# State's product of the next tile made beside the own token's products, and y gated straight from its bank

## What is computed

```python
y_intra = einsum('bclmgr,bclmge,bcmgerp->bclgep', sg, dg, xgc) + einsum('bclmgr,bclmge,bcmgerp->bclgep', sb, dg, xbc)
_, Sprev = scan(lambda S, (cd, s): (cd[..., None, None] * S + s, S), zeros, (cdec, st))
y_inter = SCALE * einsum('bclgn,bclge,bcgenp->bclgep', Cc, dec_in, Sprev)
y = (y_intra + y_inter).reshape(B, T, D_INNER)
y = _rms(y * silu(z))
return y @ W_out
```

## Time and profile before

| what | value |
|---|---|
| median of three runs | 249.6 us (249.55 to 250.18) |
| the profiled execution, whole | 250.03 us |
| its span on the core | 248.2 us |
| mean granted clock of TensorE | 0.978 |
| busy share of the span: PE, DVE, ACT, POOL | 88%, 84%, 76%, 65% |
| set-up before the loop of tiles | 0 to 43 us |
| loop of tiles | 43 to 222 us |
| FFN of the last rounds and the output | 222 to 248 us |

### The profile page before, as it was taken

The page is one execution under the profiler, slowest core; times in us unless marked ns, Lnnn a source line. Parts: engine busy times, 40 slices in busy tenths (PEclk is TensorE's granted clock), DMA queues, the critical chain, the costliest instruction groups (busy, mean ns, idle before and its releaser), DMA issues. The chain is left out here.

```text
span 248.2 us, 6592 instructions
## 1 busy us (share of the span) xinstructions
PE 218.3 (88%) x1962; PEld 159.9 (64%) x1962; DVE 208.9 (84%) x646; ACT 188.6 (76%) x728; POOL 160.3 (65%) x275
## 2 busy tenths in 40 slices
PE   0895998679999999999999999999999999999930
PEld 0893443456767666768777876877687768657920
DVE  1789999987779988986999899989989997956880
ACT  2366776669988699877988798789779977989661
POOL 7433134757798698776769686968686866563530
PEclk9999799999999999999999999999999999999985
DMA  5980000000000000000000001000100110010123
GB/s 121 228 275 4 3 0 0 1 3 1 3 3 3 0 3 1 3 0 5 1 3 0 3 3 45 3 0 1 46 3 1 23 23 0 3 44 4 42 50 87
DMA packets 10199, 6.45 MB, mean 26 GB/s; under 512 B 864, under 2 KB 9856, under 8 KB 10160
## 3 DMA queue, kind: packets, MB, share of 16 engines
q1 hardware_dynamic: 10016, 5.77, 9.6%
q0 software_dynamic: 144, 0.21, 0.4%
HBM read 3.88 MB, written 2.10 MB: 24 GB/s over the span
## 5 line engine op out<-in xcount | busy, mean ns | idle before, releaser
L978 PE MATMUL bank<-x,sg 64*64 64x256 f32 x256 | 35.0, 391 | 0.6 <-DVE sg L1393 0.6
L1386 DVE TENSOR_TENSOR x<-bank,wx 128x512 f32<-128x512 f32 x32 | 21.9, 685 | 15.5 <-ACT bank L672 12.5
L672 ACT ACTIVATE bank<-bank,rsn 128x512 f32<-128x512 f32 x32 | 21.1, 658 | 17.0 <-PE bank L879 17.0
L978 PE MATMUL bank<-xg,sg 64*64 64x256 f32 x256 | 33.0, 376 | 0.0
L966 PE MATMUL pair<-x,turned_bc 64*64 64x256 f32 x224 | 29.6, 376 | 0.0
L544 POOL TENSOR_TENSOR y<-ysum,zs 128x256 f32<-128x256 f32 x32 | 23.8, 742 | 5.5 <-DVE ysum L1409 5.5
L455 POOL TENSOR_TENSOR rb<-mse,halfn 128x2 f32<-128x2 f32 x32 | 23.7, 741 | 2.5
L452 POOL TENSOR_TENSOR mse<-msb,eps_all 128x2 f32<-128x2 f32 x32 | 8.1, 253 | 25.5 <-ACT junk L663 25.4
L1071 PE MATMUL bank<-wo_sb,yt 128*128 128x128 f32 x128 | 22.7, 300 | 0.0
L1386 DVE TENSOR_TENSOR xg<-bank,wx 128x512 f32<-128x512 f32 x32 | 21.8, 680 | 0.0
L427 POOL TENSOR_TENSOR x_lo<-xnT_all,x_hi 128x128 fp32r<-128x128 f32 x32 | 14.7, 460 | 10.4 <-ACT x_hi L587 10.4
(11 more groups left out here) (195 smaller groups left out, 750.2 us busy)
## 6 DMA issues: line engine op xcount, KB each, us to landing
x_all<-x SPq DMA_DIRECT2D x16, 128.0 KB, 4.1
out<-o_all SPq DMA_DIRECT2D x14, 128.0 KB, 2.6
cm<-consts SPq DMA_DIRECT2D x1, 640.0 KB, 6.3
w_sb<-w_in SPq DMA_DIRECT2D x1, 480.0 KB, 4.0
out<-o_all SPq DMA_DIRECT2D x4, 64.0 KB, 2.1
cm<-consts POOLq DMA_DIRECT2D x1, 128.0 KB, 4.0
wo_sb<-w_out SPq DMA_DIRECT2D x1, 128.0 KB, 4.7
bcb_sb<-bc_bias SPq DMA_DIRECT2D x1, 96.0 KB, 4.6
```

What stands on the lines that cost most here:

```text
L672: nc.scalar.activation(x_ps[:], x_ps[:], ACT.Silu, scale=rsn[:, par:par + 1]).then_inc(S["x_silu"], 1)
L978: mm = nc.tensor.matmul(y_ps[half(h)], sg[half(h), a, r], rx(x, r)[half(h)], start=start, stop=stop)
L1386: vec.tensor_tensor((x1, xg)[a][:, par].rearrange("p (a e) -> p a e", e=P), x_ps[:].rearrange("p (a e) -> p a e", e=P), wx[:, par, a].unsq ...
```

## The change

Three things are changed, in the path that runs:

1. The state's product of tile n + 1 is made in `mix(n)`, between `own_token(0)` and `own_token(1)`. It opens y's bank of tile n + 1, and the products of `mix(n + 1)` add to it there. y's bank is one of two, by the parity of the tile: bank 6 or bank 2. The first one, `state_part(0)`, stands in `step(-1)`, ahead of `score(0)`.
2. `inter_ps`, ScalarE's copy of it (`zt`), VectorE's sum (`ysum`) and GpSimd's `gated` are gone. VectorE's `gated_y` multiplies y's bank by `zs` at the place where it summed.
3. The transposes of `turn` go to bank 5, which the scores use too, in place of bank 2. So `turn(n + 1)` waits for `sg_ready` n + 1, that is, for `mask(n)`. `mix(n)` waits for `p_added` at its start.

```diff
-        t_ps, inter_ps = bank[2][:, 0:DI], bank[2][:, DI:]
+        t_ps = bank[5][:, 0:DI]
-        y_ps, ffn_ps = bank[6][:, 0:DI], bank[7]
+        y_ps, ffn_ps = (bank[6][:, 0:DI], bank[2][:, 0:DI]), bank[7]
...
@@ GpSimd, step(n)
                 if within(n + 2):
                     early(n + 2, q % 2)
-                if within(n):
-                    gated(n, q, q % 2)
                 if within(n + 2):
                     token_factors(n + 2, q % 2)
...
@@ ScalarE, step(n)
                     late_yt(n - 1)
-                if within(n):
-                    state_part(n, q % 2)
...
@@ TensorE
             def turn(n, q):
                 pe.wait_ge(S["bc_turned"], n + 1)
                 pe.wait_ge(S["t_sb"], n)
-                pe.wait_ge(S["zt_sb"], max(n - 1, 0))
+                pe.wait_ge(S["sg_ready"], n)
...
+            def state_part(n):
+                if n >= NQ:
+                    pe.wait_ge(S["st_ready"], n - NQ + 1)
+                else:
+                    pe.wait_ge(S["st_zero"], 2)
+                    pe.wait_ge(t_turn[1], 3)
+                pe.wait_ge(S["t_sb"], n + 1)
+                wait_past(pe, S["y_ready"], n - 1)
+                from_state(n % 2, st[:, n % NQ], False).then_inc(S["inter_ps"], 1)
...
+                pe.wait_ge(S["inter_ps"], n + 1)
                 pe.wait_ge(S["x1_ready"], n + 1)
-                pe.wait_ge(S["ysum_ready"], n)
+                pe.wait_ge(S["y_ready"], n)
                 pe.wait_ge(S["sg_ready"], n + 1)
+                pe.wait_ge(S["p_added"], min(n, NT - NQ))
                 earlier_tokens(0)
-                state_product()
+                next_state(0)
                 earlier_tokens(1)
-                pe.wait_ge(S["p_added"], min(n, NT - NQ))
-                next_state(0)
+                next_state(1)
                 pe.wait_ge(S["xg_ready"], n + 1)
                 own_token(0)
-                next_state(1)
+                if n + 1 < NT:
+                    state_part(n + 1)
                 own_token(1).then_inc(S["y_ps"], 1)
...
@@ VectorE
-            def summed_y(n, par, general):
+            def gated_y(n, q, par, general):
                 dve.wait_ge(S["y_ps"], n + 1)
-                if not general:
-                    dve.wait_ge(S["zt_sb"], n + 1)
+                dve.wait_ge(S["zec_ready"], n + 1)
                 if not isinstance(n, int) or n >= 2:
-                    dve.wait_ge(S["y_ready"], n - 1)
-                vec.tensor_tensor(ysum[:, par], y_ps, yk[:] if general else zt[:, par],
-                                  ALU.add).then_inc(S["ysum_ready"], 1)
+                    dve.wait_ge(S["yt_ps"], n - 1)
+                    dve.wait_ge(S["ysq_done"], n - 1)
...
+                vec.tensor_tensor(y[:, par], yk[:] if general else y_ps[par], zs[:, q], ALU.mult).then_inc(S["y_ready"], 1)
...
@@ the end of the loop, VectorE and GpSimd: last_ffn
-                gated(NT - 1, NQ - 1, 1)
...
-                summed_y(NT - 1, 1, general)
+                gated_y(NT - 1, NQ - 1, 1, general)
```

59 lines of the change are left out of this document (21 added, 38 removed).

## The result

| | before | changed |
|---|---|---|
| median | 249.84 us (249.22 to 250.63, 8 runs) | 246.84 us (246.11 to 248.54, 8 runs) |
| the profiled execution, and its span | 250.03, 248.2 us | 246.15, 244.3 us |
| mean granted clock of TensorE | 0.978 | 0.971 |

The ratio is 0.9886 (95% interval 0.9854 to 0.9919): faster by 3.0 us, where 246.8 us was forecast. The total agrees to 0.04 us.

A forecast was written before the change was run, and what follows sets the result against it. TensorE was taken to bound the loop, with VectorE only 2.5 us idle in 40. Start -0.5, rounds +3.0, GpSimd +0.3 and end +0.25 make 3.05 us, 2.8 taken: 249.6 to 246.8 us, range 244.8 to 249.4.

The forecast's parts named there:

- Part 1, the packed mix: In the mix, next state's groups end early: 1.99 us to the projection, 1.17 us a round, 4.6 from tile 11.
- Part 2, the start: In tiles 0 to 10 `turn` waits behind the mask: TensorE 1.4 us late at mix(1), 0.5 at tile 14.
- VectorE's products for B and C are late too, 1.4 at mix(1): At the loop's start, VectorE's late products raise TensorE's lateness from 0.9 us at mix(0) to 1.4 at mix(1).
- the circle: Early tiles: mask's end, `turn`, mix, y's product on VectorE, next mask's end; 4.51 us a tile, bounded by the mask.
- Part 2, the rounds: In tiles 14 to 27 `turn` behind the mask leaves a round 0.85 of its 1.17 us, 3.0 us in all.
- Through that stretch its masks can't come earlier than they do: In tiles 14 to 27 VectorE's masks stay put, limiting TensorE's gain to 0.32 us at turn(20), 0.66 at turn(21).
- The first rival: VectorE isn't the limit at `turn`: 4.6 us gained, not 3.3, and nothing lost at the start; 244.9 us, chance 0.13.
- Part 3, GpSimd's relief: Without its gate GpSimd finishes earlier, each VectorE residual shortens by 0.35 us: 0.1 us a round, 0.3 in all.
- Part 4, ScalarE: ScalarE's 32 lost copies are worth nothing, but for waits of `y_turn`, up to 0.3 us, left in the range.
- It waits for TensorE or VectorE around them: ScalarE waits for TensorE or VectorE around its 32 copies of 0.39 us, so losing them is worth nothing.
- Part 5, the end: In the last tiles y no longer passes GpSimd: 0.25 us gained at y(31), nothing taken for tile 30.
- The sum: Whole kernel: -0.5 + 3.0 + 0.3 + 0.25 = 3.05 us gained, 2.8 taken because of small waits in a round.

The follow-up runs named there:

- The old order: Changed kernel with the groups of the mix ordered as before, all else kept: 249.59 us, 0.999 of before.
- the dummy gate: Changed kernel with a GpSimd product of fixed buffers, used nowhere, at the old gate's place and with its wait for y: 245.65 us, 0.984 of before.
- the second execution of the changed kernel: Profiled execution, 248.15 us, of the changed kernel timed again with nothing changed: median 246.53 us, 0.987 of before.
- ScalarE's dummy copy: Changed kernel with a ScalarE copy of a fixed buffer, used nowhere, where `zt` was made: 247.79 us, 0.993 of before.
- a second bank: Changed kernel with the transposes of B and C in two banks by parity, `turn` waiting for an older y, not the mask: 242.71 us, 0.972 of before.

## Why the prediction was right, and where it wasn't

**Part 1, the packed mix, is right.** The forecast had 1.99 us from tile 11 on; it is 1.99 everywhere. The full gain was put at 1.17 us a round; the four mixes of a round became 1.2 us shorter (9.13 to 9.16, now 7.95), and a round got 1.08. The old order, put back, shows that the order is what packs the mix.

**Part 2, the start, has the right mechanism and too small a size.** mix(0) was put 0.9 us late and is 1.10 late; mix(1) 1.4, and is 2.25; mix(8) 1.8 to 2.2, and is 2.35; tile 14 was to be 0.5 late, and is 0.90. The missing 0.85 at mix(1) came in the step "VectorE's products for B and C are late too, 1.4 at mix(1)". Two things came on top that the sum didn't have. 0.69 us are the collision of VectorE's angle instructions with GpSimd, which the dummy gate took away. 0.23 us are the lower clock in the projection ahead of mix(0), which the second execution of the changed kernel didn't have. With a set-up that was 0.07 us shorter they make up the 0.85. From there the circle kept what was lost, as forecast: mix(4) to mix(7) is 4.44 us a tile, where 4.51 was forecast, and 4.37 without the wait, where 4.36 was.

**Part 2, the rounds, had a limit that isn't there.** The step that failed is "Through that stretch its masks can't come earlier than they do", with a limit of 0.32 us at turn(20). Turn(20) came 0.73 us earlier, counted from mix(16): 15.84 before, 15.11 now. VectorE's mask(19) ended 0.46 earlier (15.37 and 14.91 after mix(16)). 0.19 of that is x1(18), which starts behind TensorE's projection and so follows its gain in tiles 16 and 17. 0.25 are the three small instructions behind mask(18) (0.91 us before, 0.66 now). What shortened them is ScalarE's relief and not GpSimd's: with ScalarE's dummy copy they take 0.95 again, with GpSimd's dummy gate 0.56. 0.32 and 0.46 make 0.78, and 0.73 was needed. So `turn` didn't wait once from tile 12 on (it starts 0.18 to 0.20 us behind the mask at its closest), where one or two waits a round were forecast. The first rival's account of the rounds was the better one: no limit at `turn`, and with it 1.17 us a round. It named contention as the reason, but I had the place wrong: I looked at the residual, and it was three instructions of 0.15 to 0.64 us.

**Part 3, GpSimd's relief, has the wrong sign.** The residual fell to 1.89 us, close to the 1.8 that were forecast, and that is worth nothing: at 2.06 a round is no longer. At the start the relief makes VectorE 0.7 us later. The Trainium skill (SBUF — State Buffer, § SBUF: two separate sides) calls the port pair that GpSimd shares with VectorE an exclusive lock. By the same section of the Trainium skill, where VectorE's instruction has two SBUF inputs and GpSimd's reads SBUF, the one that starts first holds the pair for its whole instruction. The rows agree: VectorE's 128 x 4 instruction at 142.61 lasted to 143.25 where GpSimd's gate, at 142.49 for 0.73 us, ended at 143.22.

**Part 4, ScalarE, was mis-sized.** It was put at nothing, with waits of `y_turn` in the range only. The copy is worth 0.31 us a round, and 0.95 to 1.26 us against the two medians of the changed kernel. The step that failed is "It waits for TensorE or VectorE around them": with the dummy back, `y_turn` waits for ScalarE once a round (0.12 us), and the mask comes too late by the way through GpSimd (0.17). Whether these 0.31 us are part of the 0.47 that the old order already had isn't shown: there it is the mixes that are shorter, and the dummy copy lengthens no mix of tiles 1 to 30 (1.99).

**Part 5, the end, was put at 0.25 and gave 0.81.** From mix(28) to the end of the span it went from 44.51 to 43.70. The step that failed is that at tile 30 nothing could be had. Before, `y_turn` waited twice in the last tiles of the loop, for ScalarE and for GpSimd:

```profile
214.85 0.41 PE L1062 MATMUL bank<-cm,y 128*128 128x128 f32 x2 [0.49 <-ACT junk_o L700]
...
218.89 0.41 PE L1062 MATMUL bank<-cm,y 128*128 128x128 f32 x2 [0.47 <-POOL y L544]
```

They are the ones at tiles 29 and 30. The first is 0.11 in the changed kernel, the second:

```profile
215.13 0.41 PE L1045 MATMUL bank<-cm,y 128*128 128x128 f32 x2 [0.28 <-ACT junk_o L688]
```

That is 0.38 and 0.19 us of ScalarE's and GpSimd's relief, where the sum had nothing (Part 4 left the waits for ScalarE in the range). With ScalarE's dummy copy the first is 0.35 again. mix(30), 1.98 in place of 2.08, gave 0.10, and only 0.14 came behind mix(31), where I had put the 0.25.

**The sum.** In the profiled pair tile 14 is 0.90 us later, tiles 14 to 27 give 3.99 (forecast 3.3 with part 3) and the end 0.81: 3.9, where 3.05 was worked out and 2.8 taken. The medians differ by 3.0. They stand nearer to the forecast because the profiled execution of the changed kernel is one of its shorter ones: five of eight took 246.11 to 246.95, three 248.02 to 248.54. So the agreement to 0.04 us is partly luck: 0.4 too little loss at the start, 1.25 too little gain later, and a time of 248 us in 4 of the 13 executions, which I had not thought of.

## What to carry to other kernels

Before crediting relief on an engine off the path, look at what it will do in the time it gets: here GpSimd, freed of a gate, moved its next product beside VectorE's and held it up for 0.7 us, and with a dummy instruction and its wait in the gate's place the kernel was faster. An engine at 76% of the span can still be late once a round: ScalarE's 0.39 us a tile were worth 0.31 us a round. A new wait is to be costed with the stop that it makes on the engine behind it: this one cost 4 us where I had put TensorE late by 1.8 to 2.2 at its worst and 0.5 at tile 14, and a second bank took it away. And when a limit is given by "the mask comes at this time", ask what the mask itself follows: 0.19 of the 0.46 us by which it moved was TensorE's own gain coming round.

## What the hardware showed that I had not expected

**The same stop, two prices.** The changed kernel again, an execution of 248.15 us, by windows:

```profile
50.00:55.00 5.00, 2.73 (x39) 1.75 (x31) 4.93 (x11) 1.95 (x9) 2.87 (x6) 1.00 0.00 0
55.00:60.00 5.00, 4.82 (x43) 3.09 (x43) 2.41 (x6) 3.67 (x15) 2.86 (x6) 0.66 0.01 3
```

Here TensorE had the full clock in mix(0) and the lower one in mix(1). Its timeline:

```profile
55.18 0.41 PE L923 MATMUL pair<-cm,turned_bc 128*128 128x128 f32 x2 [2.45 <-DVE sg L1378]
...
56.45 0.69 PE L958 MATMUL bank<-x,sg 64*64 64x256 f32 x2
...
60.10 0.60 PE L1054 MATMUL bank<-wo_sb,yt 128*128 128x128 f32 x3
```

Mix(1) starts at 56.45, as in the other execution (56.55), and takes 3.65 us in place of 1.99; mix(2) is 1.56 us later, and 1.5 of it is there at the end of the span. The stops ahead of turn(1) are alike, 1.45 and 1.46 us. In one execution the lower clock falls on the projection and mix(0), of which VectorE hides all but 0.23 us; in the other on mix(1), which nothing hides. That may be what makes two groups of times, but it is shown for this one pair only. The three other long executions have no trace, and their mean granted clock is 0.963, below the 0.971 to 0.974 of the short ones beside them, where this one has 0.976.

**A 128 x 4 instruction of VectorE took 0.15 us or 0.64**, by what GpSimd did beside it.

**The score starts inside the mix.** By count, each fp32 product of 64 x 64 stands as two records in the trace: the program has 8 products on y in a tile and the trace 16 records, in steps of 0.216 us. In tile 27 above, the last step but one of the products on y starts at 195.87, the score's first records at 195.88, and the last step on y at 196.08. So the score runs beside the last products on y. If the two records of a product are one step apart, both of these products are begun before the score, and nothing overtakes. I had counted the score as work behind the mix, and a packed mix has part of it inside.
